# Transposes moved from TensorE to VectorE behind a detour through DRAM: probabilities of blocks 8 to 14 and x1 of the second stage; in the third stage the squares are loaded behind the weight codes

## What is computed

```
xl = layernorm(x)
z  = softmax(causal(xl Wq1 (xl Wk1)^T) / sqrt(32)) (xl Wv1)      one head of 512, keys <= query
x1 = LN1(xl + z)
z  = softmax((x1 Wq2)(ctx Wk2)^T / sqrt(32)) (ctx Wv2)           77 keys
x2 = LN2(x1 + z)
x3 = LN3(x2 + relu(x2 fc1 + b1) fc2 + b2)
xg = x + tanh(g_x) x3
y  = silu((LN(xg) gain + shift) dequant(q1) + b) dequant(q2) + b   512 -> 2048 -> 512
out = xg + tanh(g_f) (LN(xg) + 0.5 y)
```

## Time and profile before

| | |
|---|---|
| median of 3 runs | 1653.44 us (1651.63 to 1654.49) |
| profiled execution, its own time | 1656.21 us |
| profiled execution, its span | 1654.4 us |
| PE busy | 1617.4 us (98%), 7634 matmuls and transposes |
| DVE busy | 862.5 us (52%), 1760 instructions |
| ACT, POOL busy | 572.2 us (35%), 367.2 us (22%) |
| mean granted PE clock | 0.994 of full speed |
| DMA | 129930 packets, 70769 of them under 512 bytes, 24.5% of 16 engines' span on the queue of the data |

### The profile page before, as it was taken

How to read it: one execution, slowest core, us unless ns; L and a number is a source line. 1 busy time by engine, 2 the same in 40 slices (tenths; PEclk the granted TensorE clock), 3 DMA queues, 4 the chain that set the end, 5 groups by cost and what they waited for, 6 DMA issues and landing times. The chain is left out here.

```text
span 1654.4 us, 20692 instructions
## 1 busy us (share of the span) xinstructions
PE 1617.4 (98%) x7634; PEld 1334.5 (81%) x7634; DVE 862.5 (52%) x1760; ACT 572.2 (35%) x990; POOL 367.2 (22%) x562
## 2 busy tenths in 40 slices
PE   8999999999999999899999899999999999999999
PEld 6887888877788887678787687888888888888887
DVE  6757444477664435678888955342333232423311
ACT  5432121134221112466566533332323232323322
POOL 1212100022220100388888911000000000000000
PEclk9999999999999999799999999999999999999999
DMA  6302110131220104445545344121211112121100
GB/s 212 105 22 96 45 52 26 39 115 58 70 77 33 45 26 164 138 135 162 165 154 172 102 160 120 58 44 52 51 52 46 57 38 64 39 64 32 45 1 26
DMA packets 129930, 130.88 MB, mean 79 GB/s; under 512 B 70769, under 2 KB 70769, under 8 KB 129675
## 3 DMA queue, kind: packets, MB, share of 16 engines
q1 hardware_dynamic: 128032, 126.10, 24.5%
q10 hardware_dynamic: 1797, 3.46, 0.6%
HBM read 87.34 MB, written 42.18 MB: 78 GB/s over the span
## 5 line engine op out<-in xcount | busy, mean ns | idle before, releaser
L747 PE MATMUL banks<-split_q,split 128*128 128x512 f32 x2328 | 568.1, 393 | 4.6 <-POOL split L1563 3.2
L747 PE MATMUL banks<-split 128*128 128x512 f32 (+5 forms) x2304 | 543.1, 385 | 10.8 <-DVE split L1688 5.9
L747 PEld LDWEIGHTS banks<-split_q,split 128*128 128x128 f32 x2328 | 433.4, 188 | 96.9 <-POOL split L1563 4.1
L747 PEld LDWEIGHTS banks<-split 128*128 128x128 f32 (+3 forms) x2304 | 414.5, 185 | 107.0 <-issue 8.1
L747 PE MATMUL banks<-split,split_q 128*128 128x512 f32 (+3 forms) x1728 | 392.4, 379 | 6.8 <-DVE split_q L1688 4.1
L747 PEld LDWEIGHTS banks<-split,split_q 128*128 128x128 f32 x1728 | 308.7, 189 | 57.9 <-DVE split_q L1688 4.9
L2194 DVE TENSOR_TENSOR split<-plain,split 128x512 fp32r<-128x512 f32 x128 | 88.4, 691 | 385.6 <-ACT split L1464 385.6
L1458 ACT ACTIVATE plain<-banks,small 128x512 f32<-128x512 f32 x128 | 88.2, 689 | 400.1 <-PE banks L747 400.1
L1688 DVE TENSOR_TENSOR split<-banks,split 128x512 fp32r<-128x512 f32 (+5 forms) x232 | 146.3, 638 | 152.9 <-ACT split L1145 152.3
L1145 ACT ACTIVATE split<-banks 128x512 fp32r<-128x512 f32 (+5 forms) x232 | 124.4, 557 | 247.2 <-PE banks L957 191.1
L1497 POOL TENSOR_TENSOR small<-small 128x1 f32<-128x1 f32 x64 | 13.1, 205 | 475.7 <-DVE small L1724 475.5
(11 more groups left out here) (156 smaller groups left out, 1275.3 us busy)
## 6 DMA issues: line engine op xcount, KB each, us to landing
plain<-in_x SPq DMA_DIRECT2D x64, 256.0 KB, 2.7
xo_scratch<-plain SPq DMA_DIRECT2D x32, 256.0 KB, 2.3
x_scratch<-plain SPq DMA_DIRECT2D x32, 256.0 KB, 2.0
plain<-x_scratch SPq DMA_DIRECT2D x32, 256.0 KB, 3.0
tile_x<-xo_scratch SPq DMA_DIRECT2D x32, 256.0 KB, 3.1
xg_scratch<-tile_x SPq DMA_DIRECT2D x32, 256.0 KB, 2.1
out<-plain SPq DMA_DIRECT2D x32, 256.0 KB, 2.1
tile_x<-x_scratch SPq DMA_DIRECT2D x28, 256.0 KB, 4.6
```

What stands on the lines that cost most here:

```text
L747: mm = nc.tensor.matmul(out, left(c, l), right(c, r), start=start and c == 0 and (l, r) == PASSES[0], stop=stop and c == chunks - 1 and (l ...
```

## The change

Three parts. (1) For blocks 8 to 14 of both batches (`turned(i)`) PE no longer turns the probabilities. When exp of the block is done, SP stores each chunk into `p_scratch`, and loads it back into the same place with its 32 x 32 squares rearranged (four DMAs a chunk); DVE then turns the chunk into the PSUM bank (step "I"), and T is only the split. The order of steps in these blocks is new. (2) x1 of tiles 2 to 7 is loaded in squares in the same way (four DMAs per 128 rows), and turned by DVE; on DVE `add_y(t, 0)` moves behind the splits of x1. PE waits for the count of turns (`tp_full`) where its next turn follows one of DVE's. (3) In the first tile of the third stage `load_hb` moves from even f to the following odd f, behind the codes of that f.

```diff
+def turned(i):
+    return 8 <= i < NB - 1
+def squares_in(b, i, c):
+    return sum(turned(j) and c < chunks_of(j) for j in range(NB)) * b + sum(
+        turned(j) and c < chunks_of(j) for j in range(i + 1))
...
         n1 = chunks_of(i + 1) if i + 1 < NB else 0
         end = [(kind, i - 1, 0) for kind in "AB"]
-        if n1 > n0:
+        if turned(i) and n1 > n0:
+            g = i // 4 + 1
+            order += [("Q", g, 0), end[0], ("Q", g, 1), end[1], ("I", i, 0), ("I", i, 1), ("Q", g, 2), ("T", i, 0),
+                      ("Q", g, 3), ("T", i, 1), ("V", i, 0), ("I", i, 2), ("S", i + 1, 0), ("T", i, 2)]
+            order += [("S", i + 1, c) for c in range(1, n1)]
+            order += [("X", i + 1, 0), ("V", i, 1), ("V", i, 2)]
+        elif turned(i):
+            order += [end[0], ("S", i + 1, 0), ("S", i + 1, 1), ("I", i, 0), ("I", i, 1), ("T", i, 0), ("I", i, 2),
+                      ("S", i + 1, 2), ("T", i, 1)]
+            order += [("I", i, 3)] if n0 > 3 else []
+            order.append(end[1])
+            order += [("S", i + 1, 3)] if n0 > 3 else []
+            order += [("X", i + 1, 0), ("V", i, 0), ("T", i, 2), ("V", i, 1)]
+            order += [("T", i, 3)] if n0 > 3 else []
+            order += [("V", i, c) for c in range(2, n0)]
+        elif n1 > n0:
             g = i // 4 + 1
...
         order += [("x", b, t, 0) for t in range(AHEAD, NB)]
         for kind, i, c in ORDERS[b]:
-            if kind == "T":
+            if kind == ("I" if turned(i) else "T"):
                 order.append(("p", b, i, c))
...
+def x1b_loads(t):
+    return 16 + (t - 1) * QB * 16
...
         xo_dram = nc.dram_tensor("xo_scratch", (B * S, E), F32, kind="Internal").ap()
         xg_dram = nc.dram_tensor("xg_scratch", (B * S, E), F32, kind="Internal").ap()
+        p_dram = nc.dram_tensor("p_scratch", (C, P * 512), F32, kind="Internal").ap()
         h_dram = nc.dram_tensor("h_scratch", (TILE, E), F32, kind="Internal").ap()
...
         o_out = [sem("o_out_0"), sem("o_out_1")]
         h_out, hb_in = sem("h_out"), sem("hb_in")
+        p_out, p_in = [sem(f"p_out_{c}") for c in range(C)], [sem(f"p_in_{c}") for c in range(C)]
...
                 else:
                     sp.wait_ge(tp_full, x1_at(t - 1, k) + 1)
-                sp.dma_start(x1b[:, k], x1_dram[t * TILE + k * P:t * TILE + (k + 1) * P, :]).then_inc(x1b_in[k], 16)
+                rows = x1_dram[t * TILE + k * P:t * TILE + (k + 1) * P, :]
+                if t == 1:
+                    sp.dma_start(x1b[:, k], rows).then_inc(x1b_in[k], 16)
+                    return
+                squares_of = rows.rearrange("(q s) (c i r) -> i s c q r", q=QB, c=C, i=QB)
+                for i in range(QB):
+                    sp.dma_start(x1b[32 * i:32 * i + 32, k].rearrange("p (c q r) -> p c q r", c=C, q=QB),
+                                 squares_of[i]).then_inc(x1b_in[k], 16)
...
                     sp.dma_start(xo_dram[b * S + i * P:b * S + (i + 1) * P, :], x_shifted).then_inc(xo_stored, 16)
+                def store_p(i, c):
+                    n, at, w = squares_in(b, i, c), c * 512, width_of(i, c)
+                    if n > 1:
+                        sp.wait_ge(p_in[c], (n - 1) * QB * 16)
+                    sp.dma_start(p_dram[c, 0:P * w].rearrange("(p n) -> p n", n=w), Srow[:, i % 2, at:at + w]).then_inc(p_out[c], 16)
+                def load_p(i, c):
+                    at, w = c * 512, width_of(i, c)
+                    sp.wait_ge(p_out[c], squares_in(b, i, c) * 16)
+                    squares_of = p_dram[c, 0:P * w].rearrange("(q s c i r) -> i s c q r", q=QB, s=32, i=QB, r=32)
+                    for n in range(QB):
+                        sp.dma_start(Srow[32 * n:32 * n + 32, i % 2, at:at + w].rearrange(
+                            "p (c q r) -> p c q r", q=QB, r=32), squares_of[n]).then_inc(p_in[c], 16)
...
                     sp.dma_start(x1_dram[b * S + i * P:b * S + (i + 1) * P, :], U[:, i % 2]).then_inc(
                         x1_out[i % 2], 16)
+                    if turned(i + 2):
+                        sp.wait_ge(p_ready, b * NB + i + 2 + 1)
+                        for c in range(chunks_of(i + 2)):
+                            store_p(i + 2, c)
+                        for c in range(chunks_of(i + 2)):
+                            load_p(i + 2, c)
...
                 if f >= 8 and f % 2 == 0:
                     store_h(1, f // 2 - 4)
+                if f >= 8 and f % 2:
                     load_hb(1, f // 2 - 4)
...
                     elif kind == "Q":
                         queries(i, c)
-                    elif kind == "T":
+                    elif kind == "T" and not turned(i):
                         n = TURNS["p", b, i, c]
                         if c == 0:
                             pe.wait_ge(p_ready, b * NB + i + 1)
+                        if c == 0 and turned(i - 1):
+                            pe.wait_ge(tp_full, n)
                         pe.wait_ge(tp_free, n + 1)
...
                 pe.wait_ge(x2_ready, t * BT + k + 1)
                 pe.wait_ge(tp_free, n + 1)
+                if k == 0:
+                    pe.wait_ge(tp_full, n)
                 turn(PS[:, 2 + n % 2], lambda c: N[:, t % 2, k, c * P:(c + 1) * P])
...
                     for k in range(BT):
                         cross_values(t + 1, k)
-                if far:
-                    turn_x1(t + 2, 0)
-                    turn_x1(t + 2, 1)
                 if not ahead:
                     turn_h(0, 0)
                     turn_h(0, 1)
                 if t == 0:
                     pe.wait_ge(fcw_lo, 2 * C)
                 mlp_out(t, 0)
-                if far:
-                    turn_x1(t + 2, 2)
-                    turn_x1(t + 2, 3)
                 mlp_out(t, 1)
...
                 lo_t(n, [x1T[:, :, h, k * P:(k + 1) * P] for h in range(2)], n)
+            def turn_x1(t, k):
+                n = x1_at(t, k)
+                dve.wait_ge(x1b_in[k], x1b_loads(t))
+                dve.wait_ge(tp_full, n)
+                dve.wait_ge(tp_free, n + 1)
+                nc.vector.transpose(PS[:, 2 + n % 2], x1b[:, k]).then_inc(tp_full, 1)
...
                     elif kind == "Q":
                         lo_q(i, c)
+                    elif kind == "I":
+                        n, at, w = TURNS["p", b, i, c], c * 512, width_of(i, c)
+                        dve.wait_ge(p_in[c], squares_in(b, i, c) * QB * 16)
+                        dve.wait_ge(tp_free, n + 1)
+                        nc.vector.transpose(PS[:, 2 + n % 2, 0:w], Srow[:, i % 2, at:at + w]).then_inc(tp_full, 1)
                     elif kind == "T":
...
                     scale_w(2 * t + 1)
                 lo_probs(t + 1)
+                if far:
+                    turn_x1(t + 2, 0)
+                    turn_x1(t + 2, 1)
                 if t:
                     at = scale_y(t - 1, 3)
                     shift_y(t - 1, 3, at)
                 for k in range(BT):
                     add_z(t + 1, k)
                 if not far:
-                    stats_x3(p0, x1b, (x1b_in[0], NT * 16))
+                    stats_x3(p0, x1b, (x1b_in[0], x1b_loads(NT - 1) + 16))
                     add_y(t, 0)
...
                     return None
                 lo_x1(t + 2, 0)
+                turn_x1(t + 2, 2)
                 lo_x1(t + 2, 1)
+                turn_x1(t + 2, 3)
                 scale_w(2 * t + 1)
-                add_y(t, 0)
                 lo_x1(t + 2, 2)
                 lo_x1(t + 2, 3)
+                add_y(t, 0)
                 add_y(t, 1)
...
             def scale_w2(f):
                 if f < 4:
-                    scale_codes(*w2_stage(f), (x1b_in[f], NT * 16 + 16))
+                    scale_codes(*w2_stage(f), (x1b_in[f], x1b_loads(NT - 1) + 32))
                 else:
```

## The result

The changed kernel takes 1664.80 us (1663.68 to 1665.08, 4 runs), the kernel before in the same session 1652.93 us (1651.63 to 1654.49, 4 runs). The ratio is 1.0070, with a 95% interval of 1.0055 to 1.0085: slower by 11.9 us. Forecast were 1650.5 us, and 1640 to 1661 as the range. The prediction was wrong, in its sign and beyond its range.

The account below looks back on a forecast made before the run. PE was taken to bound attention and the second stage, with little DVE room in the latter. Attention 0, clock +1.7, second stage -1.1, third stage -3.5 gave -2.9 us: 1650.5 us against the 1653.44 median, range 1640 to 1661.

Parts of the forecast that it names:

- What goes from PE: Attention, blocks 8 to 14: turns leaving PE save 7.3 us a batch, 14.6 for both; second stage 9.6 us.
- What it costs in attention: Blocks 8 to 14: PE waits 7.3 us a batch for chunks and splits, all it gains, so net 0.
- The loads: Attention, SP's queue: each load's issue takes 0.67 us; 0.75 would bring chunk 2 0.9 us later in every block.
- +5.3: Attention's upper bound for both batches: at 0.75 us a load, waits of about 9.9 us a batch.
- The clock: Attention: block 12's 3.0 us wait brings one 3.4 us stretch at 1.2 GHz, costing +1.7 us; bounds 0 and +3.4.
- Third stage: First tile: codes issued at once, so PE's four waits go, -3.5 us; bounds -3.5 and 0.
- Second stage: Turning x1: step 0 gains 1.6 us, five steps become 0.1 longer at 32.5; -1.1 us in all.
- A: Rival, attention and second stage: waits smaller than summed, -14.4 us, 1639 us, or 1625.7 without any wait; chance 0.15.
- C: Rival, second stage: DVE sets the pace at 33.0 us a step, total about 0, 1653 us; chance 0.18.
- B had the sign: Rival, attention: SP's issues bound, loads over 0.70 us apart, clock falls in both batches; 1657.5 to 1662 us; chance 0.25.
- The rule on small pieces: Loads of probabilities: 128-byte pieces might take 7 cycles where 4 carry data; the forecast kept its 2.4 us landing.

Follow-up runs that it names:

- without the detour: Against part 1 alone: DVE turns probabilities right after exp, with no store to or load from DRAM (values of other keys); 1654.99 us, ratio 1.0011.
- with B behind exp: Against part 1 alone: no store or load of probabilities through DRAM, and step B behind the last scores and exp in four-chunk blocks; 1648.15 us, ratio 0.9963.
- part 1 alone: Against the kernel before: only the probabilities of blocks 8 to 14 turned by DVE, x1 and third stage as before; 1672.82 us, ratio 1.0117.
- the probabilities first: Against part 1 alone: SP stores and loads the probabilities of block i + 2 ahead of block i's store of x1; 1668.64 us, ratio 1.0085.
- its best order: Against part 1 alone: SP handles probabilities ahead of x1's store, and step B follows the last scores and exp in four-chunk blocks; 1652.01 us, ratio 0.9998.
- B's place alone: Against part 1 alone: only step B moved behind the last scores and exp in four-chunk blocks, SP's order kept; 1661.08 us, ratio 1.0041.
- the fastest kernel: The change with all three parts, plus SP's probabilities ahead of x1's store and step B behind last scores and exp; 1643.75 us, ratio 0.9938.

## Why the prediction was wrong

**What goes from PE: undersized, harmless.** Forecast 7.3 us a batch. By the earlier trace rows the twelve matmuls right behind a group of turns take 3.00 us, twelve others 2.88: the first one starts its successor 0.31 us later instead of 0.23. With 24 groups, 0.087 each, that is 2.1 us more: 9.4 a batch. The windows bear it out: 309.78 - 9.4 + 9.9 = 310.3 without the detour (measured 310.20), 306.3 with B behind exp (batch 0 waits 5.9; measured 306.45).

**What it costs in attention: the step that failed.** 7.3 us of waits a batch were forecast, 15.7 and 16.7 came: +17.8 for both, less the 4.2 of the step above. Of the 8.4 above the forecast in batch 0, 4.4 lie in blocks 9 to 11 and 2.2 in block 12. Three things are in it. (1) SP's queue: the diff puts the stores behind x1's store, which waits for B. I let them start at exp's end in every block. That is 2.1, 1.7 and 1.1 us late in 9, 10 and 11, where 1.3 us of waits were forecast and 5.7 came (4.0 in part 1 alone). With the probabilities first it is 2.4 there, as without any DMA if POOL's 1.1 are left aside; over all blocks it gives back 1.4 a batch. (2) DVE's queue: without any DMA PE waits 9.9 a batch, 1.1 of it by POOL's addition, where the sum gave waits to 13 and 14 (1.6) for that reason alone. I had priced the instructions right (0.65 a turn, 1.5 for B) and followed them, but in blocks 8 to 12 I let the way start at the landing of the loads; in block 8 what comes last is turns and split behind scores 1, loads or not. B's place I took for given; moved, it is worth 4.2 a batch. Blocks 13 and 14 wait 1.5 and 1.3 without DMA, forecast 0.9 and 0.7; which gaps on DVE make this 0.6 was not taken apart. Whether the turns would wait less at another place in the order was not tried. (3) POOL's addition, whose x is now loaded behind the probabilities, runs beside B or the last scores and makes one of their instructions 0.6 to 1.0 us longer: 2.2 us of waits in both batches, 5.3 of the time. The prediction counted how SP's loads delay codes, and did not ask it for this load. In block 12 of batch 0 it is 0.9, and its last loads come 1.2 later than forecast, behind one that held SP for 1.66 us: together about the 1.8 us between this wait and the forecast.

How much is the detour's and how much DVE's? With no waits part 1 alone would have gained 18.8 us, and it lost 20.4. Without the detour it lost 2.3, so 21.1 of these 39.2 us are there without any DMA, and 18.1 come with the detour in the order as written.

**The loads.** "0.67, not 0.75" was the choice, and it was right: the loads start 0.68 us apart in chains of 12 and of 16. Of the 192, four held SP for 1.4 to 1.7 us, and no other for over 0.77. That the waits were bounded by +5.3 rested on loads alone, and so the bound was no bound.

**The clock: the sign right, too small.** One stretch of 3.4 us was forecast in attention; there are 13.6 us in this execution, 6.8 lost. Between part 1 alone and its best order the stretches differ by 23.8 us in the whole execution, some 12 of the 20.8 us. Of the 23.8 us 17.0 lie in attention. In the table above longer waits go with more half clock. That the two stretches together lose 1.7 us more by the clock than before, as forecast, is luck: 6.8 are lost in attention, and 5.1 less at the entry to the second stage.

**Third stage: right. Second stage: near in its sum, wrong in its steps.** For the third stage -3.5 was forecast, measured are -4.8 in the last window and -4.0 alone. For the second the forecast was -1.1, with 1.6 gained in step 0 and 0.1 lost in each of the other five (32.5); measured are -2.1, and the six steps take 31.97, 32.08, 32.09, 32.05, 32.10 and 32.12 us, each 0.3 to 0.5 shorter. DVE is busy 28.5 us a step, where 26.75 and four turns of 0.65 make 29.4. What sets the pace at 32.1 was not taken apart.

**The rivals.** A (smaller waits) and C (steps of 33.0) did not come. B had the sign, and 0.25, but not the mechanism: it wanted loads over 0.70 us apart, and they are 0.68. What is left of the detour in a good order is 5.2 us of waits in both batches. The rule on small pieces that I had cited from the Trainium skill ("Why small descriptors are slow (HBM only)", in "DMA: Bandwidth & Descriptors") was not put to the test: no run here changed the size of the pieces. The loads landed in 2.4 us, the median, as those of the third stage had the earlier trace rows. Missing was the rival that DVE's and SP's order, as written, are the price. It could have been read from the diff.

## What to carry to other kernels

Work taken off the engine that bounds is a gain only if its new owner does it outside the way from one result to the next use; with that owner 45% busy, 24 turns a batch in its queue took all of it back, since they stand ahead of what the next softmax and the next values need. Before pricing a detour, write out each queue that it enters with everything ahead of it and behind it, also what has nothing to do with it: here a store that waited for another engine, and a load whose late landing let POOL run beside DVE and slow it. Then move what nobody waits for (B, the store of x1) behind what somebody does: that alone made +20 us of part 1 about 0.

## What the hardware showed

- A first matmul of 512 columns behind a group of turns takes 0.31 us to its successor's start, not 0.23; in blocks 8 to 14 the excess is 0.08 to 0.09 in every group, whatever the width.
- A DVE instruction with two inputs in SBUF took 1.78 us instead of 0.75 beside POOL's addition of the same size (1.87 in the kernel before); the small pass of 0.29 took 1.23.
- A load of 512 columns holds SP for 0.64 us and starts the next 0.68 us later, one of 128 columns for 0.43 and 0.47. Single loads held it for 1.4 to 1.7 us, four of 192, and what made them longer is not known; one of these makes 16 loads 11.37 us.
- Waits of 2.4 and 2.8 us went with 3.4 us at 1.2 GHz in part 1 alone and in its best order; waits of 2.7 us in the change (block 9) and in the fastest kernel (block 12) did not. In block 12 of batch 1 a wait of 1.95 us with B's place alone did, and one of 1.96 in the fastest kernel did not. Without the detour (waits up to 1.9) attention was never at half clock.
